# Joining the output stage of one transformer block and the projections of the next into one pipeline

## The chip, the cores and the metric

The kernel runs on one core of a Trainium2 chip. The metric is the device time of one execution in microseconds; three executions of the kernel before gave 4201.7, 4202.61 and 4206.91 us, median 4202.61.

## The reference

Two transformer blocks over x of shape (4, 2048, 256), 16 heads of 16. Each block adds its attention to its input and normalises (mean and variance over the 256 features, no scale or shift), then adds its feed-forward part and normalises again. Cut to what the change touches:

```
x1 = layernorm(x  + attn0(x))                 # attn0 ends with  o @ Wo0.T
x2 = layernorm(x1 + x1 @ (int4(W) + A B) + bias)
q, k = rope(x2 @ Wq.T), rope(x2 @ Wk.T);  v = x2 @ Wv.T
x3 = layernorm(x2 + attn1(q, k, v));  out = layernorm(x3 + ffn1(x3))
```

q and k go to the second attention as three bf16 parts whose sum is the float32 value. Beside them a bound on the largest squared head norms is kept, which decides whether a row maximum is needed.

## The kernel before, in words

The kernel is a row of phases, and between two phases all engines meet at a barrier: setup, `project_phase` 0, row maxima, `attend_phase` 0, `post0_phase`, `project_phase` 1, row maxima, `attend_phase` 1, `post1_phase`. Within a phase each engine has its own instruction list in a fixed order, written out by hand, and waits on counting semaphores (`Count.wait`). All DMAs are issued by SyncE (SP). PSUM has 8 banks of 128x512 float32.

Work goes over 16 groups of 512 tokens (`B * GB`). In `post0_phase` a group g is:

- step "o", PE L1119: o times Wo, 16 instructions of 256 columns, into banks Y1;
- "sum1", DVE: L1177 adds x (two halves) into rr, then `Norm.take`: L1009 statistics (4), L1013 aggregation (4); ScalarE L1018 takes the root;
- "norm1", DVE: `Norm.invert` (L1022 reciprocal, L1024 shift), then `Norm.apply`, L1029, four tensor_scalar of 128x256 that write x1;
- GpSimd L1209: x1 plus the bias gives x1b (4 of 128x256);
- "xt", PE L1126: 8 transposes of x1, copied out of PSUM by ScalarE L1152 (2 of 128x512);
- "ffn", PE L1135: x1 transposed times the folded weight wf, 16 instructions; "sum2" and "norm2", DVE: L1190 adds x1b, and the same norm gives x2, which SP L1096 stores to DRAM.

The steps of up to four groups are interleaved by `over_groups`; for DVE the order is norm1 (g-1), norm2 (g-3), sum1 (g), sum2 (g-2).

`project_phase` 1 loads x2 again (SP L329) and makes, for each group, four tiles J = q0, q1, k0, k1 of 128x512:

- PE L464: 8 transposes of x2, copied out by ScalarE L413; PE L489: q and k, 8 instructions of 512 columns each; PE L497: v, two halves of 8, through one PSUM bank, copied out by ScalarE L405;
- DVE L530 and L531: times cos and times sin (two per tile), then GpSimd L385: their sum or difference (qcos);
- the three parts: ScalarE L435 (high), DVE L539 subtracts it (rem), DVE L544 casts rem (middle), GpSimd L389 subtracts again (low), four stores of 96 KB per tile by SP L352;
- the norm bound: ScalarE L438 squares, PE L508 two bf16 matmuls per pair of tiles into bank 7, DVE L549 takes the maximum; at the end DVE L552, GpSimd L393 (all partitions) and three small DVE instructions.

Of the kernel before, what the change touches and what calls it, by code (L numbers as in the profile page):

```python
# [18 lines left out]
BF16 = mybir.dt.bfloat16  # L19
I32 = mybir.dt.int32  # L20
ACT = mybir.ActivationFunctionType
ALU = mybir.AluOpType
# [4 lines left out]
P = 128  # L27
# [1003 lines left out]


# [12 lines left out]
def post0_phase(nc, kn, w, x_d, out_d):  # L1045

    Y1, XT0, Y2 = 0, 2, 4
    with ExitStack() as ctx:
        ph = Phase(nc, ctx, "post0")
        w_in, o_in, x_in = ph.sem("w_in"), [ph.sem(f"o_in{i}") for i in range(GB)], [ph.sem(f"x_in{i}") for i in range(GB)]  # L1050
        y1, r1, y2, r2 = (ph.count(n) for n in ("y1", "r1", "y2", "r2"))
        xt_ps, xt_sb = ph.count("xt_ps"), ph.count("xt_sb")
        ab_ps, w_ffn = ph.sem("ab_ps"), ph.sem("w_ffn")
        xb = ph.count("xb")
        out = ph.stores("out_dma", 2)
        n1, n2 = Norm(ph, "n1"), Norm(ph, "n2")
        wo = ph.sb("wo", [P, DC, D])
        a_s = ph.sb("a", [16, D])
        b_s = ph.sb("b", [16, D])
        wf = ph.sb("wf", [P, DC, D])  # L1060
        bias = ph.sb("bias", [P, D])
        o_s = ph.sb("o", [P, GB, DC, TG])
        xs = ph.sb("x", [P, GB, TT, D])
        rr = ph.sb("rr", [P, 2, TT, D])
        x1 = ph.sb("x1", [P, 2, TT, D])
        x1b = ph.sb("x1b", [P, 2, TT, D])
        xt = ph.sb("xt", [P, 2, DC, TG])
        rr2 = ph.sb("rr2", [P, 2, TT, D])
        x2 = ph.sb("x2", [P, 2, TT, D])
# [3 lines left out]
        def rows(d, b, gq):  # L1073
            return d[bass.ds(b * T + gq * TG, TG), :].rearrange("(t p) d -> p t d", p=P)

        def load(sp, b, gq):
            sp.dma_start(o_s[:, gq], kn["o_d"][bass.ds(b * D, D), gq * TG:(gq + 1) * TG].rearrange("(c p) t -> p c t", p=P)).then_inc(o_in[gq], 16)
            sp.dma_start(xs[:, gq], rows(x_d, b, gq)).then_inc(x_in[gq], 16)

        @block.sync  # L1080
        def _(sp):
            for dst, src in ((wo, w["wo"]), (a_s, w["a"]), (b_s, w["b"]), (bias, w["bias"])):
                sp.dma_start(dst[:], src).then_inc(w_in, 16)
            for gq in range(GB):
                load(sp, 0, gq)
            out.start(sp)

            def do(step, b, gq, g):
                if step == "load":

                    if b + 1 < B:
                        r1.wait(sp, g * 2 + 1)
                        load(sp, b + 1, gq)
                else:
                    n2.out.wait(sp, g)
                    out.done(sp.dma_start(rows(out_d, b, gq), x2[:, gq % 2]), gq % 2)  # L1096

            over_groups(sp, ("0load", "3store"), do)
            for u in range(2):
                out.wait(sp, u, B * GB // 2 - 1)  # L1100

        @block.tensor
        def _(pe):
            for c in (y1, xt_ps, y2):
                c.start(pe)
            pe.wait_ge(w_in, 64)
            for c in range(DC):
                pe.matmul(ps[:, Y2 + c, 0:D], a_s[:, c * P:(c + 1) * P], b_s[:], start=True, stop=True).then_inc(ab_ps, 1)
            pe.wait_ge(w_ffn, DC)
            def do(step, b, gq, g):  # L1110
                u = gq % 2
                if step == "o":
                    pe.wait_ge(o_in[gq], 16 * (b + 1))
                    for half in range(2):

                        r1.wait(pe, (g - 1) * 2 + half)
                        for t in range(2 * half, 2 * half + 2):
                            for c in range(DC):
                                mm = pe.matmul(ps[:, Y1 + half, (t % 2) * D:(t % 2 + 1) * D], o_s[:, gq, c, t * P:(t + 1) * P], wo[:, c, :], start=c == 0, stop=c == DC - 1)  # L1119
                        y1.done(mm)  # L1120
                elif step == "xt":
                    n1.out.wait(pe, g)
                    for c in range(DC):
                        xt_sb.wait(pe, (g - 1) * DC + c)
                        for t in range(TT):
                            mm = pe.transpose(ps[:, XT0 + c, t * P:(t + 1) * P], x1[:, u, t, c * P:(c + 1) * P], kn["ident"][:])  # L1126
                        xt_ps.done(mm)
                else:
                    xt_sb.wait(pe, g * DC + DC - 1)
                    for half in range(2):  # L1130
                        r2.wait(pe, (g - 1) * 2 + half)
                        for t in range(2 * half, 2 * half + 2):
                            y = ps[:, Y2 + half, (t % 2) * D:(t % 2 + 1) * D]
                            for c in range(DC):
                                mm = pe.matmul(y, xt[:, u, c, t * P:(t + 1) * P], wf[:, c, :], start=c == 0, stop=c == DC - 1)  # L1135
                        y2.done(mm)

            over_groups(pe, ("0o", "1xt", "2ffn"), do)

        @block.scalar  # L1140
        def _(act):
            xt_sb.start(act)
            n1.start(act=act)
            n2.start(act=act)
            def do(step, b, gq, g):
                u = gq % 2
                if step == "xt":
                    for c in range(DC):
                        xt_ps.wait(act, g * DC + c)

                        y2.wait(act, (g - 2) * 2 + 1)
                        xt_sb.done(act.activation(xt[:, u, c], ps[:, XT0 + c], ACT.Copy))  # L1152
                elif step == "root1":
                    n1.take_root(act, g, u, kn["eps"][:, 0:1])
                else:
                    n2.take_root(act, g, u, kn["eps"][:, 0:1])

            over_groups(act, ("1xt", "0root1", "2root2"), do)

        @block.vector  # L1160
        def _(dve):
            for c in (r1, r2):
                c.start(dve)
            n1.start(dve=dve)
            n2.start(dve=dve)
            dve.wait_ge(w_in, 64)
            for c in range(DC):
                dve.wait_ge(ab_ps, c + 1)
                dve.tensor_tensor(wf[:, c], ps[:, Y2 + c, 0:D], kn["w4"][:, c], ALU.add).then_inc(w_ffn, 1)
            def do(step, b, gq, g):  # L1170
                u = gq % 2
                if step == "sum1":
                    dve.wait_ge(x_in[gq], 16 * (b + 1))
                    for half in range(2):
                        y1.wait(dve, g * 2 + half)
                        ts = slice(2 * half, 2 * half + 2)
                        r1.done(dve.tensor_tensor(rr[:, u, ts], ps[:, Y1 + half].rearrange("p (t d) -> p t d", t=2), xs[:, gq, ts], ALU.add))  # L1177
                    n1.take(dve, g, u, lambda t: rr[:, u, t], lambda t: r1.wait(dve, g * 2 + t // 2))
                elif step == "norm1":
                    n1.invert(dve, g, u)  # L1180

                    xt_ps.wait(dve, (g - 2) * DC + DC - 1)
                    xb.wait(dve, g - 2)
                    n1.apply(dve, g, u, lambda t: x1[:, u, t], lambda t: rr[:, u, t])
                elif step == "sum2":
                    xb.wait(dve, g)
                    for half in range(2):
                        y2.wait(dve, g * 2 + half)
                        ts = slice(2 * half, 2 * half + 2)
                        r2.done(dve.tensor_tensor(rr2[:, u, ts], ps[:, Y2 + half].rearrange("p (t d) -> p t d", t=2), x1b[:, u, ts], ALU.add))  # L1190
                    n2.take(dve, g, u, lambda t: rr2[:, u, t], lambda t: r2.wait(dve, g * 2 + t // 2))
                else:
                    n2.invert(dve, g, u)
                    out.wait(dve, u, b * (GB // 2) + gq // 2 - 1)
                    n2.apply(dve, g, u, lambda t: x2[:, u, t], lambda t: rr2[:, u, t])

            over_groups(dve, ("1norm1", "3norm2", "0sum1", "2sum2"), do)

        @block.gpsimd
        def _(pool):  # L1200
            xb.start(pool)
            pool.wait_ge(w_in, 64)
            def do(step, b, gq, g):
                u = gq % 2

                n1.out.wait(pool, g)
                r2.wait(pool, (g - 2) * 2 + 1)
                for t in range(TT):
                    ins = pool.tensor_tensor(x1b[:, u, t], x1[:, u, t], bias[:], ALU.add)  # L1209
# [345 lines left out]
```

## Time and profile before

| | us |
|---|---|
| median of three runs | 4202.61 |
| the profiled execution, its own time | 4210.31 |
| its span in the trace | 4208.5 |
| first DMA of post0_phase | 2311.64 |
| first DMA of project_phase 1 | 2510.96 |
| first DMA of the second attention | 2807.91 |

The profile gives, for each engine, its busy time and the start and length of each instruction from the span's start. PE is TensorE's matmuls, PEld its weight loads, DVE VectorE, ACT ScalarE, POOL GpSimd, SP SyncE; SPq rows are DMA issues. Rows of the timeline merge neighbouring instructions of one kind (x8), and their length runs from the first start to the last end. [...]

### The profile page before, as it was taken

Reading aid. Unit: us, or ns where it says so; the run is one execution under the profiler, and the core shown is the slowest. Engines: PE = TensorE matmul, PEld = TensorE weight load, DVE = VectorE, ACT = ScalarE, POOL = GpSimd, SP = SyncE. Lnnn points to the kernel's source line nnn. Section 1 sums busy time; section 2 is a strip of 40 time slices with the busy share of each in tenths; the row PEclk is TensorE's granted clock in tenths of the full one; section 3 lists DMA queues with packets and bytes.
Section 4 is the critical chain, followed back from the end, with each engine's and each line's share of the span. In section 5 each row is a group of like instructions: output and inputs, shape, how many; then the busy total and the mean of one; then the engine's idle time right before and its main releaser. Section 6 shows DMA issues by size and latency. Waiting matters only on the chain. (4 is left out here: it accounts for less than half of the span.)

```text
span 4208.5 us, 61509 instructions
## 1 busy us (share of the span) xinstructions
PE 3719.3 (88%) x21948; PEld 1426.6 (34%) x21958; DVE 2746.0 (65%) x4740; ACT 3380.6 (80%) x2758; POOL 455.1 (11%) x407
## 2 busy tenths in 40 slices
PE   6969999998998999999997858759999999999687
PEld 2432322322332322232232644422222222222565
DVE  5647888778888777888877878952323233232688
ACT  2439999999999999999998113439999999999233
POOL 3530000000000000000000216730000000000232
PEclk9989999999999999999999989979999999999899
DMA  5861111111112111211110535652212222221331
GB/s 163 257 208 56 48 57 54 45 40 57 59 47 60 45 45 46 60 48 58 54 45 15 165 122 153 190 162 69 80 58 81 68 74 77 69 81 38 112 91 50
DMA packets 281330, 348.02 MB, mean 83 GB/s; under 512 B 39310, under 2 KB 214510, under 8 KB 280753
## 3 DMA queue, kind: packets, MB, share of 16 engines
q1 hardware_dynamic: 281012, 343.97, 27.2%
q8 instruction: 176, 2.88, 0.3%
q14 instruction: 142, 1.16, 0.1%
HBM read 215.56 MB, written 128.25 MB: 82 GB/s over the span
## 5 line engine op out<-in xcount | busy, mean ns | idle before, releaser
L842 DVE SCALAR_TENSOR_TENSOR att_prob<-att_tanh,alpha,ps 128x512 f32<-128x512 f32 x2176 | 1506.5, 740 | 410.4 <-ACT att_tanh L786 367.4
L726 PE MATMUL ps<-att_q,att_k 99*128 99x512 bf16 (+5 forms) x5120 | 1135.0, 351 | 114.1 <-DMA att_v<-v_ones 56.3
L755 PE MATMUL ps<-att_prob,att_v 128*32 128x512 f32 (+3 forms) x10240 | 1162.4, 540 | 2.0 <-ACT att_prob L795 1.9
L786 ACT ACTIVATE att_tanh<-ps,rbeta 128x2048 f32<-128x2048 f32 x544 | 1125.6, 2069 | 35.8 <-PE ps L726 35.8
L795 ACT ACTIVATE att_prob<-att_prob 128x2048 f32<-128x2048 f32 x544 | 1095.6, 2014 | 1.5 <-DVE att_prob L842 1.3
L792 ACT ACTIVATE att_prob<-ps 128x1024 f32<-128x1024 f32 x1088 | 1054.3, 1021 | 25.9 <-PE ps L726 10.0
L736 PE MATMUL ps<-att_f,att_g 75*128 75x512 bf16 (+3 forms) x2560 | 810.9, 354 | 133.1 <-DVE att_prob L842 121.3
L726 PEld LDWEIGHTS ps<-att_q,att_k 96*128 96x128 bf16 (+1 forms) x5120 | 399.4, 98 | 962.7 <-ACT att_prob L792 428.1
L831 DVE TENSOR_TENSOR att_prob<-att_prob,keep 128x512 f32<-128x512 f32 (+1 forms) x320 | 187.4, 586 | 580.3 <-ACT att_prob L792 579.1
L736 PEld LDWEIGHTS ps<-att_f,att_g 75*128 75x128 bf16 x2560 | 231.7, 97 | 927.6 <-DVE att_prob L842 906.8
L755 PEld LDWEIGHTS ps<-att_prob,att_v 128*32 128x32 f32 x10240 | 216.1, 108 | 347.9 <-ACT att_prob L792 141.6
L1209 POOL TENSOR_TENSOR post_x1b<-post_x,post_bias 128x256 f32<-128x256 f32 x64 | 46.5, 757 | 2167.3 <-DVE post_x L1029 2167.3
L389 POOL TENSOR_TENSOR proj_parts<-proj_rem,proj_parts 128x512 bf16<-128x512 f32 (+2 forms) x176 | 230.6, 1312 | 132.3 <-DVE proj_parts L544 91.8
L1018 ACT ACTIVATE post_n_sd<-post_n_mv,eps 128x4 f32<-128x4 f32 x64 | 18.9, 295 | 249.9 <-DVE post_n_mv L1013 249.9
L738 PE MATMUL ps<-mask_kq,identb 128*128 128x128 bf16 x1024 | 212.5, 221 | 0.0
L811 DVE STREAM_TRANSPOSE att_ot<-ps 128x512 f32<-128x512 f32 x128 | 91.1, 712 | 180.4 <-PE ps L755 180.4
L1432 POOL TENSOR_SCALAR post_prev<-post_xt,post_om 128x512 f32<-128x512 f32 x64 | 56.9, 906 | 1172.0 <-issue 1128.9
L544 DVE CAST proj_parts<-proj_rem 128x512 bf16<-128x512 f32 (+2 forms) x176 | 162.6, 925 | 0.0
L405 ACT ACTIVATE proj_vs<-ps 128x512 f32<-128x512 f32 x64 | 38.2, 597 | 114.7 <-DMA v_ones<-proj_vs 65.7
L489 PE MATMUL ps<-proj_xt,proj_wq 128*128 128x512 f32 x256 | 127.2, 644 | 0.7 <-ACT proj_xt L413 0.7
L1029 DVE TENSOR_SCALAR post_x<-post_rr,post_n_rs,post_n_nb 128x256 f32<-128x256 f32 x256 | 122.2, 539 | 7.4
L497 PE MATMUL ps<-proj_wv,proj_xt 128*128 128x256 f32 x512 | 123.4, 384 | 3.0 <-ACT proj_vs L405 2.9
(130 smaller groups left out, 2450.6 us busy)
## 6 DMA issues: line engine op xcount, KB each, us to landing
v_ones<-proj_vs SPq DMA_DIRECT2D x128, 256.0 KB, 3.3
att_v<-v_ones SPq DMA_DIRECT2D x128, 256.0 KB
att_k<-k_parts SPq DMA_DIRECT2D x128, 192.0 KB
att_q<-q_parts SPq DMA_DIRECT2D x128, 192.0 KB
att_k<-k_parts SPq DMA_DIRECT2D x128, 128.0 KB
att_q<-q_parts SPq DMA_DIRECT2D x128, 128.0 KB
o_t<-att_on SPq DMA_DIRECT2D x512, 32.0 KB, 1.7
post_o<-o_t SPq DMA_DIRECT2D x32, 512.0 KB, 5.1
```

Source lines behind the costliest of these rows:

```text
L389: low.done(pool.tensor_tensor(parts[0:n, rp, 2], rem[0:n, r], parts[0:n, rp, 1], ALU.subtract))
L489: mm = pe.matmul(ps[0:n, PRJ0 + r], lhs, xt[:, u, c], start=c == 0, stop=c == DC - 1)
L544: mid.done(dve.tensor_copy(parts[0:n, rp, 1], rem[0:n, r]))
L726: mm = pe.matmul(ps[:, bank, col:col + w], keys, q_s[:, n % QU, h, q0:q0 + w], start=True, stop=True)
L736: mm = pe.matmul(ps[:, E0 + h % 2, col:col + w], g_s[:, c % KU, (kb % CB) * P:(kb % CB + 1) * P], f_s[:, n % QU, h, q0:q0 + w], start=True ...
L738: mm = pe.matmul(ps[:, E0 + h % 2, col:col + P], kn["identb"][:], kn["mask_kq"][:], start=False, stop=True)
L755: mm = pe.matmul(ps[VW * h:VW * (h + 1), O0 + n % 2, q0:q0 + w], v_s[:, c % KU, kb % CB, h * VW:(h + 1) * VW], prob[:, S % R, h, col:col + ...
L786: th.done(act.activation(tanh_s[:, S % 2], ps[:, QK0:QK0 + HQ], ACT.Tanh, scale=kn["rbeta"][:, 0:1]))
L792: pr.done(act.activation(prob[:, S % R, 2 * pair:2 * pair + 2], ps[:, bank:bank + 2], ACT.Exp, scale=float(HD) ** -0.5))
L795: pr.done(act.activation(prob[:, (S - 1) % R], prob[:, (S - 1) % R], ACT.Exp))
L831: kept.done(dve.tensor_tensor(block, block, kn["keep"][:].unsqueeze(1).unsqueeze(1).to_broadcast([P, 2, len(masked), P]), ALU.min))
L842: sc.done(dve.scalar_tensor_tensor(prob[:, S % R, h], tanh_s[:, S % 2, h], kn["alpha"][:, 0:1], ps[:, E0 + h % 2], ALU.mult, ALU.add))
```

## The change

`post0_phase` and `project_phase` 1 are replaced by one `middle_phase`. It has 19 iterations i; iteration i works on group i (Wo, first norm, feed-forward matmul), i-1 (second sum and norm, transposes of x2), g = i-2 (q, k, v) and i-3 (what is left of the splits of the k tiles). x2 is still stored to DRAM, for the last phase, but is no longer loaded for the projections: they read it from SBUF. Both norms are applied by ScalarE (`apply_act`), and the middle part is also a ScalarE copy in place of the DVE cast L544. `project_phase` 0 is unchanged. The numbers of instructions, matmuls and stores per group are otherwise as before. Two PSUM banks Y serve both Wo and the feed-forward matmul, two XT both transposes, two PRJ (four before) the q and k tiles, one v, one the norm bound. x and o have three buffers.

```diff
+    def apply_act(self, act, g, u, dst, src):
+        self.shift.wait(act, g)
+        for t in range(TT):
+            ins = act.activation(dst(t), src(t), ACT.Identity, scale=self.rs[:, u, t:t + 1], bias=self.nb[:, u, t:t + 1])
+        self.out.done(ins)
...
+            def project(J):
+                mul.wait(pe, J // 2 * 2 - 1)
...
+            def values(g, half):
+
+                v_sb.wait(pe, g * 2 + half - 1)
+                v_ps.done(token_rows(VB, xt2[:, g % 2], wv, half))
...
+            for i in range(NG + 3):          # PE
+                g = i - 2
+                if has(g):
+                    t2_sb.wait(pe, g * DC + DC - 1)
+                    project(4 * g)
+                    project(4 * g + 1)
+                if has(i):
+                    for half in range(2):
+                        r2.wait(pe, (i - 1) * 2 + half)
+                        y1.done(token_rows(Y + half, o_s[:, i % QU], wo, half))
+                if has(g):
+                    values(g, 0)
+                if has(i - 1):
+                    transposes(x2[:, (i - 1) % 2], n2.out, ...)
+                if has(g):
+                    values(g, 1)
+                if has(i - 3):
+                    norms(i - 3, 1)
+                if has(g):
+                    project(4 * g + 2)
+                if has(i):
+                    transposes(x1[:, i % 2], n1.out, ...)
+                if has(g):
+                    project(4 * g + 3)
+                if has(i):
+                    t1_sb.wait(pe, i * DC + DC - 1)
+                    for half in range(2):
+                        r1.wait(pe, i * 2 + half)
+                        y2.done(token_rows(Y + half, xt1[:, i % 2], wf, half))
+                if has(g):
+                    norms(g, 0)
...
+            for i in range(NG + 3):          # ScalarE, k = 4 * (i - 3)
+                high(k + 2), high(k + 3), squares(k + 2), squares(k + 3)
+                n2.take_root(act, i - 1, ...)
+                middle(k + 2), middle(k + 3)
+                n2.apply_act(act, i - 1, ...)
+                high(4 * g), high(4 * g + 1), values(g, 0)
+                copies(xt2[:, (i - 1) % 2], t2_ps, t2_sb, i - 1)
+                squares(4 * g), squares(4 * g + 1)
+                n1.take_root(act, i, ...)
+                values(g, 1)
+                n1.apply_act(act, i, ...)
+                middle(4 * g), middle(4 * g + 1)
+                copies(xt1[:, i % 2], t1_ps, t1_sb, i)
...
+            for i in range(NG + 3):          # DVE
+                largest(i - 3, 0)
+                # sum2 and n2.take of group i - 1
+                remainder(k + 2), remainder(k + 3)
+                turn(4 * g)
+                n2.invert(dve, i - 1, u)
+                turn(4 * g + 1)
+                # sum1 and n1.take of group i
+                remainder(4 * g), remainder(4 * g + 1)
+                n1.invert(dve, i, v)
+                largest(i - 3, 1)
+                turn(4 * g + 2), turn(4 * g + 3)
...
+            for i in range(NG + 3):          # GpSimd
+                rotate(k + 2), rotate(k + 3), lowest(k), lowest(k + 1)
+                rotate(4 * g), rotate(4 * g + 1), lowest(k + 2), lowest(k + 3)
+                # x1b of group i
```

The loops of the last three engines are written here in short form, in their order. `high` is L435, `squares` L438, `middle` takes the place of L544, `values` L497 and L405, `turn` L530 and L531, `remainder` L539, `rotate` L385, `lowest` L389, `largest` L549. SP issues per iteration: the loads of group i+2, the stores of q of i-3, of x2 of i-1, of k of i-3, and of v of i-2. `largest` of a pair waits for `norms` of that pair, `project(J)` for the turns of the pair before it.

## Rows read from the trace of the kernel before

**Rows 1.** Stretches: length, busy PE, PEld, DVE, ACT, POOL; clock, DMA share, GB/s
```profile
2307.00:2506.00 199.00, 144.94 (x644) 121.48 (x644) 167.55 (x514) 28.62 (x65) 46.54 (x64) 0.89 0.43 127
2506.00:2808.00 302.00, 211.53 (x694) 120.07 (x704) 246.70 (x298) 104.07 (x192) 182.67 (x129) 0.88 0.61 179
2633.50:2649.60 16.10, 13.88 (x43) 7.88 (x44) 15.34 (x19) 6.52 (x12) 11.62 (x8) 0.89 0.67 196
2649.60:2665.80 16.20, 12.46 (x44) 7.16 (x44) 15.33 (x19) 6.43 (x12) 11.62 (x8) 1.00 0.68 195
```

**Rows 2.** Timeline of one group of post0_phase: start us, us, what, x count
```profile
2403.42 1.28 DVE L1177 TENSOR_TENSOR post_rr<-ps,post_x 128x512 f32<-128x512 f32 x2
2404.62 1.39 DVE L1009 BATCH_NORM_STATS2 post_n_st<-post_rr 128x6 f32<-128x256 f32 x4
...
2406.16 0.38 DVE L1013 BATCH_NORM_AGGREGATE post_n_mv<-post_n_st 128x2 f32<-128x6 f32 x4
...
2409.46 0.14 DVE L1022 RECIPROCAL post_n_rs<-post_n_sd 128x4 f32<-128x4 f32 x1
...
2409.94 1.38 DVE L1029 TENSOR_SCALAR post_x<-post_rr,post_n_rs,post_n_nb 128x256 f32<-128x256 f32 x4
...
2411.71 2.96 DVE L1029 TENSOR_SCALAR post_x<-post_rr,post_n_rs,post_n_nb 128x256 f32<-128x256 f32 x4
```

**Rows 3.** Timeline of one group of project_phase 1, PE and SP
```profile
2641.07 1.04 PE L464 MATMUL ps<-ident,proj_xs 128*128 128x128 f32 x8
...
2642.23 0.52 SPq L329 DMA_DIRECT2D proj_xs<-x  x1
...
2649.91 0.60 PE L508 MATMUL ps<-proj_sqr,headsum 128*128 128x512 bf16 x2 [2.20 <-DVE proj_nrm L549]
...
2650.35 3.60 PE L489 MATMUL ps<-proj_xt,proj_wq 128*128 128x512 f32 x8
...
2653.78 1.89 PE L497 MATMUL ps<-proj_wv,proj_xt 128*128 128x256 f32 x8
...
2658.38 0.51 SPq L329 DMA_DIRECT2D proj_xs<-x  x1
```

**Rows 4.** Timeline of project_phase 1, GpSimd beside DVE
```profile
2654.02 1.45 POOL L385 TENSOR_TENSOR proj_qcos<-proj_qcos,proj_qsin 128x512 f32<-128x512 f32 x1
2654.26 1.75 DVE L539 TENSOR_TENSOR proj_rem<-proj_qcos,proj_parts 128x512 f32<-128x512 f32 x1
...
2657.24 0.68 DVE L549 TENSOR_REDUCE proj_nrm<-ps 128x1 f32<-128x512 f32 x1
2657.84 0.67 DVE L530 TENSOR_TENSOR proj_qcos<-ps,proj_cos 128x512 f32<-128x512 f32 x1
```

**Rows 5.** Groups by line and form: busy us, mean ns, idle before
```profile
L544 DVE CAST proj_parts<-proj_rem 128x512 bf16<-128x512 f32 x64 | 81.3, 1272 | 0.0
L539 DVE TENSOR_TENSOR proj_rem<-proj_qcos,proj_parts 128x512 f32<-128x512 f32 x64 | 72.8, 1138 | 16.5 <-ACT proj_parts L435 16.5
L1029 DVE TENSOR_SCALAR post_x<-post_rr,post_n_rs,post_n_nb 128x256 f32<-128x256 f32 x128 | 66.3, 579 | 4.0
```

**Rows 6.** ScalarE's groups by form, whole span
```profile
L435 ACT ACTIVATE proj_parts<-proj_qcos 128x512 bf16<-128x512 f32 x64 | 40.6, 634 | 80.3 <-POOL proj_qcos L385 80.3
...
L1018 ACT ACT_TABLE_LOAD x18 | 23.1, 1283 | 16.8 <-PEq L130 16.5
...
L1018 ACT ACTIVATE post_n_sd<-post_n_mv,eps 128x4 f32<-128x4 f32 x64 | 18.9, 295 | 249.9 <-DVE post_n_mv L1013 249.9
...
L191 ACT ACTIVATE setup_sc<-setup_sc 128x2 f32<-128x2 f32 x1 | 0.2, 204 | 7.1 <-DMA setup_sc<-in_scalars 7.1
```

**Rows 7.** Timeline near the ends of the two phases
```profile
2489.87 1.97 PE L1126 MATMUL ps<-ident,post_x 128*128 128x128 f32 x8 [5.29 <-DVE post_x L1029]
...
2491.63 8.80 PE L1135 MATMUL ps<-post_wf,post_xt 128*128 128x256 f32 x32
...
2798.33 0.37 POOL L393 PARTITION_ALL_REDUCE proj_top<-proj_top  x1 [6.74 <-issue]
```

More of the change, by code:

```diff
@@ L1084, in _, with load @@
[L1084 to L1098, printed above, removed]
+            def load(g):
+                b, gq = divmod(g, GB)
+                sp.dma_start(o_s[:, g % QU], kn["o_d"][b * D:(b + 1) * D, gq * TG:(gq + 1) * TG].rearrange("(c p) t -> p c t", p=P)).then_inc(o_in[g % QU], 16)
+                sp.dma_start(xs[:, g % QU], rows(x_d, g)).then_inc(x_in[g % QU], 16)
@@ new lines, in store @@
+            def store(J):
+                g, (kind, m) = J // 4, (("q", 0), ("q", 1), ("k", 0), ("k", 1))[J % 4]
+                low.wait(sp, J)
+                for q in range(NHQ):
+                    row = g * D + q * (HQ * HD) + m * VW
+                    sp.dma_start(kn[f"{kind}_d"][:, row:row + VW, :].rearrange("k r t -> r k t"),
+                                 parts[q * VW:(q + 1) * VW, J % RP]).then_inc(parts_out[J % RP], 16)
+            v_out.start(sp)
+            x_out.start(sp)
@@ L1140, in _ @@
         @block.scalar
         def _(act):
-            xt_sb.start(act)
+            for c in (t1_sb, t2_sb, hi, mid, sq, v_sb):
+                c.start(act)
             n1.start(act=act)
             n2.start(act=act)
[L1145 to L1156, printed above, removed]
@@ L1158, in _, with high, squares, middle @@
-            over_groups(act, ("1xt", "0root1", "2root2"), do)
+            def high(J):
+                stored(act, J - RP)
+                rot.wait(act, J)
+                hi.done(act.activation(parts[:, J % RP, 0], qcos[:, J % R], ACT.Copy))
+            def squares(J):
+                norm.wait(act, (J - R) // 2)
+                sq.done(act.activation(sqr[:, J % R], qcos[:, J % R], ACT.Square))
+            def middle(J):
+                rest.wait(act, J)
+                mid.done(act.activation(parts[:, J % RP, 1], rem[:, J % R], ACT.Copy))
@@ L1165, in _ @@
             n2.start(dve=dve)
[L1166 to L1173, printed above, removed]
-                    for half in range(2):
[L1175 to L1186, printed above, removed]
-                    for half in range(2):
[L1188 to L1195, printed above, removed]
@@ L1199, in _ @@
         @block.gpsimd
         def _(pool):
[L1201 to L1209, printed above, removed]
-                xb.done(ins)
-            over_groups(pool, ("1bias",), do)
+            for c in (rot, low, xb):
+                c.start(pool)
```

304 lines of the change are left out of this document (241 added, 63 removed).

## The prediction

> **What bounds the kernel now.** The stretch to read is from the first DMA of post0_phase at 2311.64 us to the first DMA of the second attention at 2807.91: 496.3 us, 11.8% of the span. Outside it the change alters nothing, so the question is how long the joined phase takes in its place.
>
> First the busy times of the two phases. In both DVE is the fullest engine: 167.6 of 199 us and 246.7 of 302; PE follows with 145 and 212 at a granted clock of 0.89 and 0.88; ScalarE is nearly idle, 29 and 104 us, and GpSimd has 47 and 183 [rows 1]. So each phase is bound by DVE, and PE, second in each, waits. Then the timelines: two loads of x2 are 16.15 us apart, which is one group of project_phase 1 [rows 3]; post0_phase takes 199 us for its 16 groups with both its ends, and about 11.2 us a group between them (the sum that starts at 2403.42 [rows 2] starts again at 2414.59 for the next group). Together 27.3 us a group.
>
> Third, what DVE spends there that isn't work. The cast to the middle part has a mean of 1272 ns and the subtraction 1138 ns, where the same kind of pass out of PSUM takes 0.67 [rows 4, 5]. The timeline shows why: the subtraction that began at 2654.26 ended at 2656.01, half a microsecond after the GpSimd instruction beside it (2654.02 to 2655.47) [rows 4]. Four norm applications take 1.38 us for x1 and 2.96 for x2, while GpSimd makes x1b [rows 2].
>
> **The work of one group in the joined phase.** Durations are start to start.
>
> PE: eight q, k or v instructions' worth are 3.43 us (2653.78 - 2650.35) [rows 3]; q, k, v, Wo and the feed-forward matmul are five such: 17.15. Two sets of transposes, 1.04 each, and two pairs of bound matmuls, 0.43 each (2650.35 - 2649.91) [rows 3]: 20.1 us at the full clock.
>
> DVE loses the casts (81.3 us over 16 groups, 5.1 each) and the applications (66.3, 4.1 each) [rows 5]. What is left: sum, statistics and aggregation of a norm are 1.20 + 1.54 + 0.38 = 3.12, inversion 0.48, twice each [rows 2]; eight rope products at 0.60, two maxima at 0.60 [rows 4], four subtractions of 0.6 to 1.14: about 18 us. GpSimd stays at 14.4 ((46.5 + 182.7)/16). ScalarE had (28.6 + 104.1)/16 = 8.3 and gets four casts of 0.63 [rows 6] and eight applications. No row has an ACTIVATE with two pointer operands. From below it costs as one without: 204 ns for 2 elements; with one pointer it is 295 for 4; the 512-element copy is 634, so an element is some 0.83 ns [rows 6]. For 256 elements that makes 0.42 us without, 0.60 with two pointers, and neighbours overlap by about 0.1. I take 0.60, since both operands are pointers: four in 2.1 us (bounds 1.4 and 2.4). ScalarE's sum is some 15 us. DMA: 0.43 x 199 / 16 = 5.3 and 0.68 x 16.1 = 10.9 us of engine time a group [rows 1], less the reload of x2: under 16 us. So PE is the fullest, and no sum exceeds 20.1.
>
> **The period of the joined loop.** Each engine's list is fixed, so I follow one iteration, with 0 where PE ends the bound matmuls `norms(g, 0)` of the iteration before. DVE waits for exactly that: `largest` is first in its list.
>
> DVE: 0.17 for PE's tail (3.60 - 3.43 [rows 3]), maximum 0.60, sum and statistics of the second norm 3.12: 3.9. Then two subtractions. GpSimd has by then done the two low parts in front (rotations end near 0.3, two of 1.5 more: 3.4), so 0.60 each: 5.1. Rope product pair 6.3, inversion 6.8, second pair 8.0, sum and statistics of the first norm 11.1. Two more subtractions, now beside GpSimd's `lowest(k+2)` and `(k+3)`: between 1.14, the mean, and 1.75, the row above [rows 4, 5], I take 1.3 each: 13.7. Inversion 14.2. ScalarE applies: 16.3. PE: transposes 1.04, k1 1.72, feed-forward 3.43, bound matmuls 0.43: 22.9.
>
> A second path must be looked at, since one PSUM bank serves both halves of v. ScalarE applies the second norm from 6.8 to 8.9; its two high parts wait for the GpSimd rotation (8.0 + 1.3) and end at 9.9; the copy of v's first half at 10.5; only then PE does the second half (12.2), bound matmuls, k0: 14.4. PE thus waits for the transposes' input from 14.4 to 16.3; the path through DVE decides. In all PE idles 0.3 + 0.6 + 1.9 us. ScalarE's squares and copies (to 13.4) and its last two casts and copies fit before PE needs them (16.3 + 1.1 + 1.1 against 16.3 + 1.04 + 1.72). SP issues 23 DMAs of about 0.5, loads two groups ahead: hidden.
>
> The gap of 1.9 us is nearly the 2.2 us that stands before L508 now; there neighbouring groups show 0.89 and 1.00 [rows 1, 3]. A group at 0.89 spends 1.8 us more at the lower clock than at the upper and loses 0.9 us of PE's work. At about every second iteration that adds 0.4. **Period: 23.3 us**, against 27.3 now. Bounds: all four subtractions at 0.60 gives 22.2, as the path through PE then decides; all at 1.75 gives 26.1.
>
> [...]
>
> **Ends of the loop.** Iterations 3 to 15 are full: 13 x 23.3 = 302.9.
> - Start: Wo can begin when its weights and the first o have landed; they are issued first, about 5.4 us from 2311.64.
> - i = 0: a pure chain. Wo at the lower clock 6.9, the A B matmuls and the two adds 3, sum and statistics 3.1, root and inversion 0.8, application 2.1, then transposes after an idle stretch of 5 us, at half speed as at 2489.87 (1.97), copies 0.7, and 3.43 + 1.9 for the feed-forward matmul (there 32 took 8.80 where 6.86 is full speed) [rows 7]: 24.
> - i = 1: both norms in a row with two applications on ScalarE, no q: 18. i = 2: the full path without the leftovers of i-3: 21.3.
> - i = 16: no first norm; up to k1, 17.6. i = 17: 14.6.
> - Tail: turns, rotations, high parts, subtractions, casts, low parts of the last k pair on GpSimd until 9.8, then the all-partition maximum, in front of which GpSimd stands idle for 6.74 us today [rows 7], 0.4, and 9.2 as today from its end to the next first DMA (2798.33 + 0.37 to 2807.91): 26.2.
>
> Sum: 5.4 + 24 + 18 + 21.3 + 302.9 + 17.6 + 14.6 + 26.2 = 430.0 us in place of 496.3: 66.3 less. The profiled execution took 4210.31, so 4144.0 for it; the median shown is 7.7 below that execution: **4136.3 us**.
>
> **Rivals.**
> - PE becomes the true bound: the waits above overlap better than I think, the period is 20.1 to 22. For it: no engine's sum but PE's exceeds 19. Against: `largest` at the head of DVE's list ties both norms, one after the other, into the loop. 13 x 1.3 to 3.2 less: 4094 to 4119. Chance 0.12.
> - [...] Period 24.4 to 27: 4150 to 4184. Chance 0.27.
> - Slower: Identity needs another activation table than Sqrt. ScalarE would load twice per norm, four times per iteration, 1.283 us each [rows 6], all inside the chain root, inversion, application: 5.1 us on the period and some 14 in the short iterations, 80 us: 4216. It decides from a period of 28.4 (66.3/13 = 5.1 over mine). For it: 18 loads stand at the root in this kernel, where post1_phase mixes it with a sigmoid. Against: post0_phase mixes root and Copy with a single load, project_phase 1 adds Square with none. Chance 0.06. [...]
> - Not quite as bad, a period of 27 to 28.9 by several waits at once: about no change, 0.05.
>
> My own case, period 22.2 to 24.4, 4122 to 4150, has 0.5. Under 0.2% (8.4 us) this kernel's measurement can't tell from no change. Faster by more than that 0.90, within 0.03, slower 0.07. The range 4108 to 4176 leaves out about half of the first rival, the end of the second and the slower cases.
>
> **What would show it.** In the trace after: the same PE line every 23.3 us in the full iterations, DVE with no cast and no norm application in this stretch, ScalarE's application at 0.6 us x256, no ACT_TABLE_LOAD after the first in the phase; PE waiting before the transposes of x1 for ScalarE some 2 us, and before v's second half 0.6; DVE waiting for PE at `largest`; granted clock 0.95 or more; the phase 430 us long. I am wrong if ScalarE's list, not DVE's, is what PE waits for (its application comes late because the queue in front of it is long), if the clock sinks below 0.9, or if the application costs much over 0.6.

## The result and the profile after

The changed kernel takes 4128.18 us (median; 4127.06 to 4128.79), the kernel before beside it 4203.77 (4201.7 to 4206.91). The ratio is 0.9817, 95% interval [0.9805, 0.983]: 75.6 us less. Forecast were 4136.3 and a range of 4108 to 4176.

The profiled execution took 4128.27 us, its span is 4125.7. From the first DMA of the joined phase (2310.73) to the first DMA of the second attention (2725.52) are 414.8 us, where 496.3 stood before and 430.0 were forecast. The windows view of the changed kernel, the whole phase first, then one full iteration (columns as in [rows 1]):

```profile
2311.00:2735.00 424.00, 344.24 (x1337) 234.96 (x1353) 260.19 (x617) 232.42 (x451) 200.22 (x193) 0.92 0.65 171
2554.00:2576.00 22.00, 20.54 (x84) 14.07 (x84) 15.65 (x39) 14.30 (x28) 12.34 (x14) 1.00 0.73 190
```

In the full iterations PE is the fullest engine, 20.5 of 22.0 us, at a granted clock of 1.00, full speed, where DVE was in both phases before [rows 1]. DVE has 15.7, ScalarE 14.3. The timeline of that iteration, cut to its chain (start us, us, what; in brackets the idle time in front and who ended it):

```profile
2553.78 3.60 PE L1173 MATMUL ps<-mid_xt,mid_wq 128*128 128x512 f32 x8
2553.98 0.69 DVE L1347 TENSOR_REDUCE mid_nrm<-ps 128x1 f32<-128x512 f32 x1 [1.40 <-PE ps L1187]
...
2557.62 1.26 DVE L1342 TENSOR_TENSOR mid_rem<-mid_qcos,mid_parts 128x512 f32<-128x512 f32 x2
...
2560.48 2.07 ACT L1035 ACTIVATE mid_x<-mid_rr,mid_n_nb,mid_n_rs 128x256 f32<-128x256 f32 x4 [0.93 <-DVE mid_n_nb L1024]
...
2563.24 0.63 ACT L1247 ACTIVATE mid_parts<-mid_qcos 128x512 bf16<-128x512 f32 x1 [0.17 <-POOL mid_qcos L1410]
...
2564.41 1.99 PE L1157 MATMUL ps<-mid_wv,mid_xt 128*128 128x256 f32 x8 [0.71 <-ACT mid_vs L1268]
...
2564.64 1.89 DVE L1342 TENSOR_TENSOR mid_rem<-mid_qcos,mid_parts 128x512 f32<-128x512 f32 x2
...
2565.21 1.16 ACT L1252 ACTIVATE mid_sqr<-mid_qcos 128x512 bf16<-128x512 f32 x2
...
2566.25 0.30 ACT L1018 ACTIVATE mid_n_sd<-mid_n_mv,eps 128x4 f32<-128x4 f32 x1
2566.44 0.60 ACT L1268 ACTIVATE mid_vs<-ps 128x512 f32<-128x512 f32 x1
...
2566.80 0.16 DVE L1024 SCALAR_TENSOR_TENSOR mid_n_nb<-mid_n_mv,mid_n_rs 128x4 f32<-128x4 f32 x1
...
2567.08 2.07 ACT L1035 ACTIVATE mid_x<-mid_rr,mid_n_nb,mid_n_rs 128x256 f32<-128x256 f32 x4
...
2569.20 1.09 PE L1165 MATMUL ps<-ident,mid_x 128*128 128x128 f32 x8 [0.65 <-ACT mid_x L1035]
...
2571.85 3.62 PE L1157 MATMUL ps<-mid_wf,mid_xt 128*128 128x256 f32 x16
...
2575.74 3.60 PE L1173 MATMUL ps<-mid_xt,mid_wq 128*128 128x512 f32 x8
```

First and last row are the same line one iteration apart: 21.96 us. PE waits twice for ScalarE: 0.71 us before the second half of v, for the copy of its first half, and 0.65 before the transposes of x1, for the norm's application. The root of the first norm starts only at 2566.25, as the squares stand in front of it in ScalarE's list. The application at 2567.08 has two things in front of it that end within 0.1 us of each other: ScalarE's second copy of v at 2567.04 and DVE's inversion at 2566.96. Subtractions that lie beside GpSimd take 1.89 for two, the others 1.26, against 1138 ns each before [rows 5]. By groups (form, count, busy us, mean ns, idle in front):

```profile
L1035 ACT ACTIVATE mid_x<-mid_rr,mid_n_nb,mid_n_rs 128x256 f32<-128x256 f32 x128 | 66.4, 589 | 17.5 <-DVE mid_n_nb L1024 17.0
...
L1018 ACT ACT_TABLE_LOAD x1 | 1.3, 1283 | 23.4 <-DVE mid_n_mv L1013 23.4
...
L1342 DVE TENSOR_TENSOR mid_rem<-mid_qcos,mid_parts 128x512 f32<-128x512 f32 x64 | 53.8, 877 | 3.9 <-ACT mid_parts L1247 3.9
```

One application costs 589 ns on ScalarE, against 579 on DVE [rows 5]: the work isn't cheaper there, it is elsewhere. And the whole phase loads an activation table once. In the short iterations at the end the waits are longer; the timeline of the changed kernel:

```profile
2672.38 1.09 PE L1165 MATMUL ps<-ident,mid_x 128*128 128x128 f32 x8 [3.50 <-ACT mid_x L1035]
2674.18 3.64 PE L1157 MATMUL ps<-mid_wv,mid_xt 128*128 128x256 f32 x8 [0.70 <-ACT mid_vs L1268]
...
2684.35 5.37 PE L1173 MATMUL ps<-mid_xt,mid_wq 128*128 128x512 f32 x8 [2.24 <-DVE mid_qsin L1336]
...
2694.97 3.48 PE L1157 MATMUL ps<-mid_wv,mid_xt 128*128 128x256 f32 x8 [3.53 <-ACT mid_vs L1268]
```

After these waits of 2.24 and 3.53 us PE needs 5.37 and 3.48 us for what takes 3.60 and 1.99 in the full iteration; the granted clock was 0.67 from 2684.35 to 2689.55 us and 0.54 from 2694.9 to 2698.3. After the wait of 3.50 the transposes still take their usual 1.09, at 1.00; only the half of v behind them is slow, 3.64, at 0.56 (2674.1 to 2678.0).

### The profile page after: what moved, and what is told of

The parts are those of the page before. It is cut to its first block and busy times, and to the rows that moved or that the text cites. A ratio compares the mean times of both kernels' runs of the same rounds, so it can differ in the third digit from the quotient of the medians.

```text
span 4125.7 us, 61470 instructions
## 1 busy us (share of the span) xinstructions
PE 3703.2 (90%) x21943; PEld 1418.7 (34%) x21958; DVE 2592.8 (63%) x4548; ACT 3478.9 (84%) x2950; POOL 425.9 (10%) x407
## 5 line engine op out<-in xcount | busy, mean ns | idle before, releaser
L1436 POOL TENSOR_TENSOR mid_x1b<-mid_x,mid_bias 128x256 f32<-128x256 f32 x64 | 44.5, 731 | 2127.4 <-ACT mid_x L1035 2127.4
L389 POOL TENSOR_TENSOR proj_parts<-proj_rem,proj_parts 128x512 bf16<-128x512 f32 (+2 forms) x112 | 131.5, 1176 | 129.0 <-DVE proj_parts L544 89.9
L446 ACT ACTIVATE proj_parts<-ps 128x512 bf16<-128x512 f32 (+1 forms) x96 | 57.2, 596 | 75.4 <-PE ps L489 63.9
L1018 ACT ACTIVATE post_n_sd<-post_n_mv,eps 128x4 f32<-128x4 f32 x32 | 9.4, 293 | 123.5 <-DVE post_n_mv L1013 123.5
L1247 ACT ACTIVATE mid_parts<-mid_qcos 128x512 bf16<-128x512 f32 x64 | 40.1, 626 | 78.9 <-POOL mid_qcos L1410 78.7
L738 PEld LDWEIGHTS ps<-mask_kq,identb 128*128 128x128 bf16 x1024 | 101.2, 99 | 2.6 <-issue 0.7
L539 DVE TENSOR_TENSOR proj_rem<-ps,proj_parts 128x512 f32<-128x512 f32 (+1 forms) x96 | 66.0, 687 | 54.0 <-ACT proj_parts L446 50.2
L1525 PE MATMUL ps<-post_mix,post_wk 128*128 128x512 f32 x128 | 62.9, 637 | 40.5 <-DVE post_rr L1636 34.5
```

What stands on the lines that cost most here:

```text
L389: low.done(pool.tensor_tensor(parts[0:n, rp, 2], rem[0:n, r], parts[0:n, rp, 1], ALU.subtract))
L738: mm = pe.matmul(ps[:, E0 + h % 2, col:col + P], kn["identb"][:], kn["mask_kq"][:], start=False, stop=True)
L1525: mm = pe.matmul(ps[:, KV + m], wk[:, c, m * P:(m + 1) * P], mix[:, u, 1, c], start=c == 0, stop=c == DC - 1)
```

## The experiments

All kernels compute everything. Times are medians, each beside runs of the kernel before on the same chip; "period" is the distance of the same PE line in two full iterations.

**1. The moves without the join.** The two phases stay as they were; both norms' applications and the cast to the middle part go to ScalarE.

```diff
 # post0_phase, DVE
-                n1.apply(...), n2.apply(...)
+                n1.invert(...), n2.invert(...)
 # post0_phase, ScalarE
+                n1.apply_act(...), n2.apply_act(...)
 # project_phase 1: from DVE (tensor_copy) to ScalarE, behind high and square of the next tile
+                if rope and s > L_HI:
+                    J = s - L_HI - 1
+                    rest.wait(act, J)
+                    mid.done(act.activation(parts[:, J % RP, 1], rem[:, J % R], ACT.Copy))
```

> The kernel before, still in two phases, with both norms applied by ScalarE in post0_phase and the cast to the middle part done by ScalarE in project_phase 1. Theory (the gain comes from taking work off DVE, the join adds the overlap of the two phases' different fullest engines and saves the gap between them): post0_phase falls from 11.2 us a group to 9, project_phase 1 from 16.1 to 13.5, together 22.5 against 21.95 of the joined loop; the gap between the phases of some 15 us stays. Total 75 less than before plus about 0: 4130 to 4150. Rival A (the join is what pays): less than a third of the 76 us comes from this, 4180 or more. Rival B (the join pays nothing): at or under the joined kernel, 4128 or less.

Measured: 4164.73 us (4161.34 to 4165.26), ratio 0.9898 [0.9882, 0.9915], so 41 us less than before. A group of the first phase takes 9.62 us, one of the second 14.9, by the stores of x2 and loads of x on SP's queue in the timeline:

```profile
2406.49 0.36 SPq L1106 DMA_DIRECT2D x<-post_x  x1
...
2416.11 0.36 SPq L1106 DMA_DIRECT2D x<-post_x  x1
...
2641.82 0.51 SPq L329 DMA_DIRECT2D proj_xs<-x  x1
...
2656.54 0.49 SPq L329 DMA_DIRECT2D proj_xs<-x  x1
```

It fell between the two theories, and 14.9 is over the sum of any engine. The view of waits from 2520 to 2700 us names what neither had (who waits, for whom: us in total, times, longest):

```profile
ACT proj_vs L405 <- DMA v_ones<-proj_vs: 43.2, 11, 5.5
...
PE ps L501 <- ACT proj_vs L405: 17.3, 11, 2.1
```

ScalarE's copy of v waits for the store of v two groups earlier to free one of two buffers, 3.9 us a group, and with ScalarE stand the high parts and casts, and PE. Experiment 5 takes that up.

**2. The join without the moves, and with one of them.** The joined phase, with the applications and the cast back on DVE (join_alone), the applications alone (join_dve_apply), or the cast alone (join_dve_cast).

```diff
 # join_alone and join_dve_apply: ScalarE
-                n2.apply_act(act, i - 1, ...), n1.apply_act(act, i, ...)
 # DVE, where it inverted
-                n2.invert(dve, i - 1, u), n1.invert(dve, i, v)
+                n2.apply(dve, i - 1, u, ...), n1.apply(dve, i, v, ...)
 # join_alone and join_dve_cast: from ScalarE's list to DVE's
-                middle(k + 2), middle(k + 3), middle(4 * g), middle(4 * g + 1)
+            def middle(J):
+                rest.wait(dve, J)
+                mid.done(dve.tensor_copy(parts[:, J % RP, 1], rem[:, J % R]))
```

> The joined phase with both norm applications and the middle cast back on DVE. Theory: DVE's sum per group is again 16 + 4.1 + 5.1, some 26 us with GpSimd's hold-ups, so DVE bounds the loop and the period is 26 to 27.5 us where it is 21.95: 65 to 85 us slower than the joined kernel, 4190 to 4210, about the kernel before. Rival A (the join pays): a period of 24 or less, 4155 or less.

> The joined phase with the cast on ScalarE, the norm applications on DVE (1.4 us for four alone, up to 3 beside GpSimd, against 2.07 on ScalarE). Theory (one chain through DVE's list sets the period): the second norm's application now stands in front of the second pair of rope products, which adds 1.4 to 2.9, the first norm's is 0.7 shorter if GpSimd is idle: period 22.7 to 24.2, 4138 to 4157. Rival (PE and ScalarE's queue set the period): 22 or less, 4128 or less, since ScalarE gets 4.1 us lighter.

> The joined phase with the norms on ScalarE, the middle cast on DVE (0.4 us alone, 1.27 mean before). Theory (the DVE chain): four casts more in the chain, 1.6 to 5 us: period 23.6 to 27, 4150 to 4193, and GpSimd's low part takes 1.5 us again instead of 1.2 since DVE's cast holds it up. Rival (slack of DVE, 6 us a period, takes them): 22 to 22.5, 4128 to 4136.

Measured, beside before at 4206.03:

- join_alone: 4182.35 (4179.7 to 4183.2), ratio 0.9942 [0.9925, 0.9958], period 25.7 on the mean (24.6 to 26.9).
- join_dve_apply: 4177.71 (4174.32 to 4178.77), ratio 0.9932 [0.9916, 0.9949], period 25.2 on the mean (23.4 to 26.3).
- join_dve_cast: 4144.65 (4141.7 to 4147.97), ratio 0.9852 [0.9835, 0.9868], period 23.15.

Each kernel is set against its own runs of before: the changed one gains 75.6 us, join_dve_apply 28.3, join_dve_cast 61.4. So on the joined phase the applications are worth 47 us and the casts 14. The first was expected at 10 to 29; the second, and join_alone, came out faster than expected (4144.7 against 4150 to 4193, 4182.4 against 4190 to 4210). The timeline of join_dve_apply says why the applications weigh so much:

```profile
2562.14 2.14 DVE L1029 TENSOR_SCALAR mid_x<-mid_rr,mid_n_rs,mid_n_nb 128x256 f32<-128x256 f32 x4
...
2567.56 0.58 ACT L1268 ACTIVATE mid_vs<-ps 128x512 f32<-128x512 f32 x1
...
2568.19 3.37 PE L1157 MATMUL ps<-mid_wv,mid_xt 128*128 128x256 f32 x8 [2.76 <-ACT mid_vs L1268]
```

DVE's application pushes the rope products back behind it, with them GpSimd's rotation, ScalarE's high parts, which wait for the rotation, and the copy of v behind these. PE waits 2.76 us for that copy, and then the next eight matmuls take 3.37 us, where the same line takes 1.99 in the changed kernel. The granted clock was 0.58 there (2568.1 to 2571.6 us). The delay of DVE is paid for twice, the second time through the clock. In join_dve_cast the casts take 0.38 us each where no GpSimd instruction lies beside them, not the 1272 ns of [rows 5], and GpSimd's low part stays at 1.14: the expected slow-down of GpSimd isn't there. The cost, 1.2 us of period, shows in two waits of PE for the applications: 0.72 before the transposes of x2, where the changed kernel has none, and 1.18 in place of 0.65 before those of x1. The timeline of join_dve_cast:

```profile
2575.34 1.09 PE L1165 MATMUL ps<-ident,mid_x 128*128 128x128 f32 x8 [0.72 <-ACT mid_x L1035]
...
2582.47 1.09 PE L1165 MATMUL ps<-ident,mid_x 128*128 128x128 f32 x8 [1.18 <-ACT mid_x L1035]
```

**3. ScalarE's list: is it what PE waits for?** The period is 21.95, not 23.3, and both waits of PE are for ScalarE. Four kernels change orders alone; the first three also put DVE's inversion of the first norm in front of its two subtractions:

```diff
 # invert_first, chain_first, chain_values: ScalarE
-                squares(4 * g), squares(4 * g + 1)
                 n1.take_root(act, i, ...)
+                squares(4 * g), squares(4 * g + 1)         # invert_first
                 values(g, 1)
                 n1.apply_act(act, i, ...)
 # chain_first and chain_values: squares and values(g, 1) go behind n1.apply_act
 # the same three: DVE
+                n1.invert(dve, i, v)
                 remainder(4 * g), remainder(4 * g + 1)
-                n1.invert(dve, i, v)
 # chain_values and dve_apply_values (this one on join_dve_apply): ScalarE
+                values(g, 0)
                 high(4 * g), high(4 * g + 1)
-                values(g, 0)
```

> The joined kernel; ScalarE takes the first norm's root in front of the two squares, and DVE inverts in front of the two subtractions it now does first. Theory of the prediction (the path through DVE's list sets the period): the inversion is done 0.9 us earlier, PE's transposes of x1 come that much earlier as far as PE is ready, 0.65 us: period 21.3 instead of 21.95. Rival, from the trace after (ScalarE's queue ties with DVE's): the squares and the second v copy still stand in front of the application on ScalarE and end at the same time as before, so it starts at 13.3 us into the iteration either way: 21.9, no change.

> As invert_first, and on ScalarE the first norm's root and application both stand in front of the two squares and the second copy of v. If the norm chain is what PE waits for in front of the transposes of x1: the application starts 1.1 us earlier, the wait of 0.65 us goes, period 21.3, 8 to 10 us less in all than the joined kernel. If PE's own list is the limit there already: no change.

> As chain_first, and ScalarE copies the first half of v out of its PSUM bank in front of the two high parts, which wait for GpSimd's rotations. PE's second half of v then starts right behind the transposes, 0.7 to 0.9 us earlier. Theory (two paths, one through the norm, one through the v bank): period 20.9 to 21.0, the transposes of x1 wait again for the norm, 0.3 to 0.6 us; 14 us less than the joined kernel. Rival (the high parts then come late for DVE's subtractions): no gain over chain_first.

> join_dve_apply (norms applied by DVE) with the same edit on the copy of v. There PE waited 2.76 us in front of v's second half, behind the high parts that waited for a late rotation, and TensorE's clock fell. Theory (the v bank turned DVE's delay into PE's): the wait goes, the period falls from about 25.1 to 22.5 to 23, 4141 to 4148 in all. Rival (DVE's list itself is the limit there): 24.5 or more, 4165 or more.

Measured, beside before at 4205.04:

- invert_first: 4122.88 (4122.05 to 4123.71), ratio 0.9805 [0.9785, 0.9825], period 21.80.
- chain_first: 4127.03 (4126.71 to 4128.51), ratio 0.9816 [0.9799, 0.9832], period 21.89.
- chain_values: 4119.44 (4118.76 to 4121.6), ratio 0.9796 [0.978, 0.9813], period 21.77.
- dve_apply_values: 4158.85 (4157.54 to 4160.16), ratio 0.989 [0.9871, 0.991], period 24.7 on the mean (23.3 to 26.4).

invert_first decides between DVE and ScalarE. The timeline of its ScalarE, in an iteration whose q starts at 2550.39:

```profile
2561.81 0.31 ACT L1018 ACTIVATE mid_n_sd<-mid_n_mv,eps 128x4 f32<-128x4 f32 x1
2562.00 1.16 ACT L1252 ACTIVATE mid_sqr<-mid_qcos 128x512 bf16<-128x512 f32 x2
2563.04 0.60 ACT L1268 ACTIVATE mid_vs<-ps 128x512 f32<-128x512 f32 x1
2563.54 2.06 ACT L1035 ACTIVATE mid_x<-mid_rr,mid_n_nb,mid_n_rs 128x256 f32<-128x256 f32 x4
```

The root comes 11.42 us after q, before 12.47: 1.05 earlier. The application comes after 13.15 instead of 13.30: 0.15 earlier. Between them stand the squares and the copy of v, back to back. DVE's inversion ends at 2562.53, 1.0 us before the application starts. So here it isn't the inversion that sets the start, but ScalarE's own queue. In the changed kernel the two tie, and taking the inversion away leaves the queue. (invert_first has two runs; its intervals overlap those of the changed kernel, and whether it is faster isn't shown.) chain_first takes these two away from there; the wait before the transposes goes, and a new one stands before the feed-forward matmul, since the copies of the transposes now come last:

```profile
2569.37 3.72 PE L1157 MATMUL ps<-mid_wf,mid_xt 128*128 128x256 f32 x16 [0.54 <-ACT mid_xt L1262]
```

chain_values ends the wait before v's second half too, and the two that are left are 0.47 and 0.71, both on ScalarE:

```profile
2566.33 1.09 PE L1165 MATMUL ps<-ident,mid_x 128*128 128x128 f32 x8 [0.47 <-ACT mid_x L1035]
...
2569.86 3.72 PE L1157 MATMUL ps<-mid_wf,mid_xt 128*128 128x256 f32 x16 [0.71 <-ACT mid_xt L1262]
```

The periods of chain_first and chain_values missed what was expected (21.3, and 20.9 to 21.0): each order freed one instruction and made another late. ScalarE works there for 11 us (2558.77 to 2569.8) with one gap of 0.52, so what counts is which of its instructions PE wants first.

dve_apply_values gives back 18 of join_dve_apply's 47 us. Its time lies between its theory and the rival, its period with the rival (24.5 or more). The wait for the copy of v is gone, as the theory had it, but another takes its place: in the waits view from 2400 to 2650 us PE waits for DVE's own application.

```profile
PE ps L1165 <- DVE mid_x L1029: 29.0, 10, 3.2
```

**4. The order after PE's wants.** copies_early takes chain_values and puts the copies of x1's transposes ahead of v's second copy and of the casts. copies_early_largest also moves DVE's `largest(i-3, 0)` behind the second norm's statistics, to test the forecast's claim that `largest` at the head of DVE's list ties the loop.

```diff
 # copies_early: ScalarE, on chain_values
                 n1.apply_act(act, i, ...)
                 squares(4 * g), squares(4 * g + 1)
+                copies(xt1[:, i % 2], t1_ps, t1_sb, i)
                 values(g, 1)
                 middle(4 * g), middle(4 * g + 1)
-                copies(xt1[:, i % 2], t1_ps, t1_sb, i)
 # copies_early_largest: also DVE
-                largest(i - 3, 0)
                 # sum2 and n2.take of group i - 1
+                largest(i - 3, 0)
```

> As chain_values, and on ScalarE the two copies of the transposed x1 stand in front of the second copy of v and the two middle parts. Theory (what the order edits ran into is ScalarE's list: 11 us without a gap from the second norm's application to these copies, PE waits 0.7 us for them in front of the feed-forward matmul): the wait goes, period 20.9 to 21.1 instead of 21.77, 4107 to 4112. Rival (DVE's chain is the limit): no more than 0.2 us a period, 4116 or more.

> As copies_early, and DVE takes the maximum behind the second norm's statistics instead of as the first thing of the iteration. The prediction held that this wait ties both norms into the loop. If so, both norms come up to 0.6 us earlier: 0.2 to 0.4 us less a period than copies_early, at or below 20.7, 3 to 6 us less in all. If PE's own work (20.1) or ScalarE is the limit: the same as copies_early within 2 us.

Measured, beside before at 4206.11: copies_early 4106.44 (4105.85 to 4108.39), ratio 0.9766 [0.975, 0.9782]; copies_early_largest 4108.51 (4105.91 to 4110.72), ratio 0.9771 [0.9755, 0.9788]. Both periods are 20.79, a little under the 20.9 to 21.1 that were expected of copies_early. The windows view of copies_early, 200 us of full iterations, then of the changed kernel, the same stretch:

```profile
2400.00:2600.00 200.00, 194.35 (x803) 135.29 (x812) 145.77 (x373) 137.90 (x271) 116.49 (x114) 1.00 0.73 204
```
```profile
2400.00:2600.00 200.00, 186.81 (x755) 127.81 (x763) 142.61 (x346) 130.39 (x255) 113.12 (x111) 1.00 0.74 192
```

PE is busy for 97% of the stretch against 93%, and one wait is left in copies_early's timeline, with no wait at the feed-forward matmul behind it:

```profile
2557.68 1.09 PE L1165 MATMUL ps<-ident,mid_x 128*128 128x128 f32 x8 [0.46 <-ACT mid_x L1035]
...
2560.33 3.62 PE L1157 MATMUL ps<-mid_wf,mid_xt 128*128 128x256 f32 x16
```

This version beats both kernels: 99.7 us under the one before, and some 22 under the changed one (99.7 against 75.6 by each one's own runs of before: 24). Moving `largest` changes nothing here. Both norms' chains do move: ScalarE's application of the second norm starts 5.67 us after q instead of 6.70. But the next thing in ScalarE's list is the copy of v's first half, and now it waits for PE. The timeline of copies_early_largest:

```profile
2552.20 0.60 ACT L1268 ACTIVATE mid_vs<-ps 128x512 f32<-128x512 f32 x1 [1.07 <-PE ps L1157]
```

So in this order `largest` doesn't tie the loop. In the changed kernel's own order the copy of v stands behind the high parts, which hang on DVE's rope products; there `largest` was not moved.

**5. The stores of v.** moves_v4 is moves_alone with four buffers for v in place of two; before_v4 gives the kernel before the same.

```diff
-        v_out = ph.stores("v_out", 2, NHQ)
+        v_out = ph.stores("v_out", VS, NHQ)          # VS = 4
-        vs = ph.sb("vs", [P, 2, TT, H, VW])
+        vs = ph.sb("vs", [P, VS, TT, H, VW])
```

> moves_alone with four buffers of v instead of two in project_phase 1. There ScalarE waited 3.7 to 5.5 us in most groups for the store of an earlier v, which stands behind the k tiles' stores in SP's list, and the group took 14.9 us. Theory (two separate phases keep a stall that the joined order has not, so part of what the join gains over the moves is this stall): 13 to 13.8 us a group, 20 to 28 us less than moves_alone, 4137 to 4145, still above the joined kernel's 4128. Rival (ScalarE would wait anyway for the rotations): within 5 us of moves_alone.

> The kernel before with four buffers of v in project_phase 1 and nothing else. Theory (the wait of ScalarE for the v stores was free there, since DVE bounds the group at 15.3 of 16.1 us busy, and came onto the path only once DVE was relieved): the waits of 65.7 us in all go from ScalarE's rows, and the time falls by no more than the idle share of DVE, 0 to 12 us: 4194 to 4206. Rival (the stall was already part of the bound before): 20 us or more less, as with moves_v4.

Measured: moves_v4 4124.45 (4122.46 to 4127.48), ratio 0.9808 [0.9792, 0.9824]: 40 us under moves_alone, and below the 4137 to 4145 that were expected. The timeline shows a group every 12.05 us in the second phase, and the windows view PE without a gap:

```profile
2607.14 2.24 SPq L363 DMA_DIRECT2D v_ones<-proj_vs  x4
...
2619.19 2.23 SPq L363 DMA_DIRECT2D v_ones<-proj_vs  x4
```
```profile
2600.00:2640.00 40.00, 39.90 (x145) 24.56 (x147) 32.50 (x47) 28.24 (x53) 36.71 (x28) 1.00 0.89 268
```

before_v4 took 4203.99 (4202.69 to 4208.04), ratio 1.0001 [0.9992, 1.0011]. In the waits of the kernel before the same stall stands, and in those of before_v4, same stretch, the first rows have no trace of it. The first block below is of before, the second of before_v4:

```profile
ACT proj_vs L405 <- DMA v_ones<-proj_vs: 42.1, 9, 5.9
```
```profile
POOL proj_qcos L386 <- DVE proj_qsin L532: 88.7, 22, 40.4
ACT proj_parts L436 <- POOL proj_qcos L386: 86.6, 40, 3.7
```

42 us of a waiting ScalarE cost nothing while DVE was the bound; what ScalarE waits for now is GpSimd and, through it, DVE. As soon as ScalarE had DVE's work, the same stall cost 40.

## Why the prediction was right, and where it wasn't

**Direction and size.** Right, and for the reason given: DVE bound both phases, the change takes its casts and applications away, and PE becomes the fullest engine. The time lies in the forecast's own case (4122 to 4150), its period (22.2 to 24.4) doesn't. Its slower rival, a table load at every root, is dead: one load of 1.283 us in the phase, as in post0_phase before (project_phase 1 had none), and 589 ns for an application that was put at 0.60 us.

**The period, 23.3 forecast and 21.95 measured: 13 x 1.35 = 17.5 us too much.** This is the term that was mis-sized, by three steps. The first norm's statistics ended 10.9 us after q, at 11.1 by the forecast; up to there the steps hold within 0.3 us. The second pair of subtractions was put at 2.6 and took 1.89. And the clock's 0.4 us for every iteration wasn't there, since PE's waits are 0.71 and 0.65 and not 1.9, and behind waits that short the granted clock was 1.00 (the changed kernel, 2400 to 2600 us). Together these are 1.3. (The clock's term was also worked out too small: [rows 1] has PE busy for 13.88 us in the group at 0.89 and 12.46 in the one at 1.00, which is 1.4 more and not 0.9. And a wait near 2.2 us doesn't settle the clock: in the kernel before, eight q instructions took 5.29 us behind waits of 2.27 and 2.30 in front of L508, at 2634.22 and 2682.62, and 3.60 behind 2.18 and 2.20, at 2585.02 and 2650.35.) The forecast's lower bound of 22.2 doesn't follow from its own working either: with all subtractions at 0.60 the chain is 1.4 shorter, 21.5, or 21.9 with the clock's 0.4. The period of 24.4 to 27, which had a chance of 0.27, didn't come.

**"The path through DVE decides", with `largest` tying the loop: right for the first part, wrong in that it decides alone.** The chain as forecast gives the application's end at 16.3, the trace has 15.4. DVE does wait for PE at `largest` (1.40), works from there without a gap, and ScalarE's application of the second norm starts on its inversion 6.7 us after q (6.8 by the forecast). From then on ScalarE works through its own list with a gap of 0.17, and this list and DVE's end within 0.1 us of each other in front of the first norm's application. The forecast named ScalarE's list as a way to be wrong, and held that its squares and copies fit. They do fit in time, but they stand in front. With root and inversion 1.0 us earlier the application came 0.15 earlier (invert_first); orders that change ScalarE's list as well brought 20.79. No run changes ScalarE's list and leaves DVE's inversion in its late place, so what that list costs by itself isn't shown.

**PE as the true bound.** That rival had 20.1 to 22 for the period, a time of 4094 to 4119 and a chance of 0.12. 21.95 lies at its edge; by the forecast's own sum this period gives 4118.8. That the time came out in the forecast's own case, 9 us above, is luck: it comes from the two errors below, the ends and the 7.7 us of the median. With the orders of copies_early, 20.79 is 0.7 over PE's sum of 20.1.

**The ends.** Forecast and measured, by the same PE lines: start 5.4 and 5.0; i = 0 24 and 22.2; i = 1 18 and 19.4; i = 2 21.3 and 20.8; i = 16 17.6 and 20.8; i = 17 14.6 and 18.2; tail 26.2 and 22.9. The misses are +6.8 for the last two iterations and -4.6 for the rest, 2.2 in all. In the last two the waits are of 2 to 3.5 us, and the granted clock falls to 0.92 (2663.5 to 2684.3 us) and 0.81 (2684.3 to 2702.7): with less of PE's own work in an iteration the chain through ScalarE and DVE lies open (no run tests this).

**The sum.** The phase was forecast at 430.0 and took 414.8, 15.2 too long. The median was missed by 8.1 only, because the 7.7 us by which the profiled execution of before lay over its median have no counterpart after (4128.27 against 4128.18): two errors of opposite sign. So the nearness of 4136.3 is in part luck too.

**What paid.** Neither part does as much alone: the moves 41 us, the join 24, both 76. The 11 that are left over look like a gain from the pair, but the four v buffers show another thing. With that stall gone the moves alone give 81.7 (ratio 0.9808, against 0.9817 for the changed kernel; the intervals overlap), at 9.62 + 12.05 = 21.7 us a group, against 21.95 joined. So a larger buffer brings the moves as far as the join does, and a gain of the join over that isn't shown. The joined kernel itself was not run with four buffers.

The join does save something, the gap between the phases, which the moves keep. The timeline of moves_v4:

```profile
2502.26 1.97 PE L469 MATMUL ps<-ident,proj_xs 128*128 128x128 f32 x8 [21.17 <-DMA proj_sin<-in_sin]
```

Yet from first DMA to first DMA moves_v4 takes 415.0 us (2309.56 to 2724.57) and the joined phase 414.8. It gives the 21 us back, a part by its longer period (0.25 x 16 = 4), the rest by elimination in its first and last iterations. And the other promise, that PE's idle time in the first phase (9.62 against 3.43 + 3.43 + 1.04 = 7.9 us of work) is filled by the other's work, isn't kept while PE waits 1.4 us for ScalarE in each iteration. copies_early collects a part: 0.9 x 16 = 14 us and some at the ends, 18.0 under moves_v4 on the same chip. Whether the two phases would gain by other orders too wasn't tried, and why the joined kernel doesn't run into the stall of v with its two buffers was not tested by itself; no row of its waits from 2400 to 2600 us is for a DMA, and its groups are 22 us apart instead of 14.9.

## What to carry to other kernels

When a full engine hands work to an idle one, read the receiver's fixed list as a chain: what the fullest engine wants first must stand first there, and here the order of the same instructions, on ScalarE and one step of DVE, was worth 22 us, nearly a third of the change. A wait that costs nothing on an idle engine is a debt that falls due when that engine gets work: look through its waits, DMA stores above all, before moving anything to it. And split a change of two ideas by both halves, with the stall of each half removed, before crediting the pair.

## What the runs showed of the hardware

- An ACTIVATE of Identity with two pointer operands took 589 ns on the mean for 256 elements, four in a row 2.07 us, and one table load of 1283 ns served it, root, copy and square in the whole joined phase (changed kernel).
- Behind a wait of 2.76 us TensorE took 3.37 us for eight matmuls that take 1.99 in the full iteration (join_dve_apply, granted clock 0.58), behind 3.53 us 3.48 (changed kernel, 0.54). Behind waits of up to 0.71 us in the changed kernel and up to 1.18 in join_dve_cast the granted clock was 1.00 from 2400 to 2600 us.
- The DVE cast of 512 elements to bf16 took 0.38 us with no GpSimd instruction beside it (join_dve_cast, 2547.71 and 2556.04 us), against 1272 ns on the mean in the kernel before [rows 5]; GpSimd's low part took 1.14 us each with and without the casts on DVE.
